# Zero-weight products of TensorE inside the value sums of the L1 attention

## What is computed

```python
qkv = hidden_states @ Wqkv                       # 512 -> 32 heads x 16 (q), 16 (k), 16 (v)
scores = einsum('bqhd,bkd->bhqk', q, k) * d**-0.5
scores = where(causal, scores + slopes * (pos_k - pos_q), -1e30)
probs = softmax(scores)
attn = einsum('bhqk,bkd->bqhd', probs, v).reshape(B, S, 512)
return attn @ Wo
```

## Time and profile before

| | |
|---|---|
| median of 3 runs | 4314.05 us (4307.27 to 4315.57) |
| the profiled execution, its own time | 4301.57 us |
| its span, first to last instruction | 4299.7 us |
| busy in the span: TensorE, VectorE, ScalarE, GpSimd | 3781.4, 2802.1, 2279.9, 1890.6 us |
| mean granted TensorE clock | 0.928 of full speed |

### The profile page before, as it was taken

One profiled execution on the slowest core, in us unless ns is written; L12 is line 12 of the kernel. 1 busy time (PEld: TensorE's weight loads), 2 busy tenths in 40 slices (PEclk: granted clock), 3 DMA queues, 4 the chain that ended last, 5 costly groups with the idle time before them and its releaser, 6 DMA issues.

```text
span 4299.7 us, 63322 instructions
## 1 busy us (share of the span) xinstructions
PE 3781.4 (88%) x21648; PEld 1877.8 (44%) x21648; DVE 2802.1 (65%) x4529; ACT 2279.9 (53%) x3945; POOL 1890.6 (44%) x1566
## 2 busy tenths in 40 slices
PE   6799987889988849999999999999999984867899
PEld 2344443223332325555455555555555552443344
DVE  6533323675567448888888898888888866565322
ACT  5522221455455546667666676667666654453222
POOL 5400000000000317778787877778787774553000
PEclk7699996789889979999999999999999997998999
DMA  3100001101000010000000000000000001012100
GB/s 109 48 1 1 0 23 27 16 1 18 16 1 1 1 57 12 21 16 13 24 1 25 12 24 13 20 18 10 27 1 24 6 25 38 23 45 67 36 10 20
DMA packets 62768, 91.28 MB, mean 21 GB/s; under 512 B 12309, under 2 KB 36392, under 8 KB 62452
## 3 DMA queue, kind: packets, MB, share of 16 engines
q1 hardware_dynamic: 62456, 87.31, 7.2%
HBM read 73.62 MB, written 6.85 MB: 19 GB/s over the span
## 4 chain that ended last, share of the span: by engine, by line
PE 65%; DVE 14%; issue 8%; ACT 6%; POOL 3%; DMA 2%; SPq 1%; DVEq 0%; POOLq 0%; ACTq 0%
PE psum L329 14%; PE psum L330 14%; PE psum L331 14%; PE psum L1370 3%; DVE arena L1519 3%; PE psum L2431 2%; PE psum L2419 2%; PE psum L1343 2%; PE psum L2427 2%; PE psum L2388 2%; PE psum L1354 2%; PE psum L2410 1%; DVE x L2116 1%; ACT xn L218 1%; PE psum L1339 1%
## 5 line engine op out<-in xcount | busy, mean ns | idle before, releaser
L329 PE MATMUL psum<-xt_hi,arena 128*128 128x512 f16 (+1 forms) x2272 | 869.9, 383 | 50.3 <-DVE arena L1509 14.2
L330 PE MATMUL psum<-xt_lo,arena 128*128 128x512 f16 (+1 forms) x2272 | 868.8, 382 | 0.0
L331 PE MATMUL psum<-xt_hi,arena 128*128 128x512 f16 (+1 forms) x2272 | 867.5, 382 | 0.0
L2214 POOL TENSOR_TENSOR arena<-arena 128x1024 f16<-128x1024 f16 x256 | 516.2, 2035 | 78.0 <-DVE arena L2026 47.1
L1288 POOL TENSOR_TENSOR rs<-sd,epsc 128x1 f32<-128x1 f32 x15 | 8.2, 548 | 1130.8 <-DVE sd L1563 1130.8
L1519 DVE TENSOR_REDUCE arena<-psum 128x1 f32<-128x512 f32 (+3 forms) x608 | 366.1, 656 | 180.7 <-PE psum L1343 179.5
L329 PE MATMUL psum<-arena 128*128 128x512 f16 (+1 forms) x1152 | 421.5, 369 | 59.0 <-DVE arena L2839 20.7
L1471 ACT ACTIVATE arena<-psum 128x512 f32<-128x512 f32 x576 | 319.7, 598 | 282.9 <-PE psum L1354 183.3
L330 PE MATMUL psum<-arena 128*128 128x512 f16 (+1 forms) x1152 | 421.1, 369 | 0.0
L331 PE MATMUL psum<-arena 128*128 128x512 f16 (+1 forms) x1152 | 420.8, 369 | 0.0
L329 PEld LDWEIGHTS psum<-xt_hi,arena 128*128 128x128 f16 x2272 | 223.9, 99 | 300.2 <-DVE arena L1505 14.6
(11 more groups left out here) (330 smaller groups left out, 7839.5 us busy)
## 6 DMA issues: line engine op xcount, KB each, us to landing
arena<-m_wi SPq DMA_DIRECT2D x64, 320.0 KB, 3.0
arena<-m_wo SPq DMA_DIRECT2D x32, 256.0 KB, 2.6
arena<-arena SPq DMA_DIRECT2D x96, 64.0 KB, 2.5
x<-L_attn_x SPq DMA_DIRECT2D x4, 1024.0 KB, 8.6
out<-x SPq DMA_DIRECT2D x4, 1024.0 KB, 4.3
arena<-gate_wT SPq DMA_DIRECT2D x16, 224.0 KB, 2.5
arena<-up_wT SPq DMA_DIRECT2D x16, 224.0 KB, 2.5
arena<-down_wT SPq DMA_DIRECT2D x14, 256.0 KB, 2.6
```

Of the source, the lines that this page charges most:

```text
L329: nc.tensor.matmul(out, lh, rh, start=start, stop=False)
L330: nc.tensor.matmul(out, lh, rl, start=False, stop=False)
L331: return nc.tensor.matmul(out, ll, rh, start=False, stop=stop)
L2214: nc.gpsimd.tensor_tensor(m4_ar[:, q], heads[q].broadcast_to([P, HG, P]), m4_le.unsqueeze(1).broadcast_to([P, HG, P]), ALU.mult).then_inc( ...
```

## The change

`add_zero(n, w)` issues n products with the zero weights `a2_z` over w columns of `a2_oh` (the output weights of the layer, any finite data would do) into the bank of the value sums, with `start=False`: they add zero to it. They are issued only while a sum is open, that is, after a value step that is not the last of its sum (`open_sums`). Ahead of each score there is one of 256 columns; ahead of a row and of an x step three of 512 columns. No position has another number of any other step, and nothing moves on another engine.

```diff
+            def add_zero(n, w):
+                for _ in range(n):
+                    nc.tensor.matmul(psum[:, 6, 0:w], a2_z, a2_oh[:, 0, 0:w], start=False, stop=True, skip_group_check=True)
+
+            open_sums = False
             for what, p, *u in STEPS2:
...
                 elif what == "row":
+                    if open_sums:
+                        add_zero(3, 4 * P)
                     e = SLOT2[what, p]
                     pe.wait_ge(a2_e, max(e, 2))
...
                 elif what == "score":
+                    if open_sums:
+                        add_zero(1, 2 * P)
                     score_unit(p, *u)
                 elif what == "value":
                     b, t = SEQ2[p]
+                    open_sums = u[0] % (t + 1) < t
...
                 elif what == "x":
+                    if open_sums:
+                        add_zero(3, 4 * P)
                     pe.wait_ge(x_norm, p + (NT * (s + 1) + 1))
```

## The result

The changed kernel takes 4376.7 us (median of 4 runs, 4366.2 to 4384.6) beside 4310.7 us for the kernel before (4 runs): a ratio of 1.0155, with a 95% interval of 1.0124 to 1.0187. It is 67 us slower. The forecast was 17 us faster, and the time lies outside the range, which ended at 4345 us.

What follows compares the result with a forecast made beforehand. TensorE was taken as busiest (89% of the stage) but slowed by half clock, its full-clock pace shared with VectorE. Terms -46 (clock) + 24 (scores) + 2 (row, x) + 3 (remaining half clock) = -17 us: median 4314 to 4297, range 4256 to 4345 us.

Steps and rivals of the forecast that it cites:

- Products ahead of scores: Added 256-column products ahead of scores: 445 at 0.108 us, bounds 0 and 48 us, half taken, +24 us.
- Rival D: Each product ahead of a score also pays its weight load: 93 us less 46 for the clock, +47, 4361 us; chance 0.06.
- Cover: Share of the products ahead of scores hidden in TensorE's slack or waits for VectorE: about half of 48 us.
- slack of 0.145 us: TensorE's spare time in each 0.60 us pair of maximum and score where VectorE sets the pace, said to cover 0.108 us.
- rival C: TensorE is the bound between its gaps, in tails' scores and dense stretches; pairs 0.70 us apart; +35, 4349 us; chance 0.20.
- Products ahead of row and x: 72 products of 512 columns, 15.5 us, mostly fill 28.2 us of waits ahead of row and x steps; +2 us taken.
- The clock: Of 218 us at half clock in the stage, two thirds, 145 us, come back at 0.32 each: -46 us.
- most begin behind a gap ahead of an x step (L1430) or a row step (L1388): Where the stage's 22 half-clock stretches were said to begin; a few behind a wait of the maxima.
- the scores around it bring more 128-row products: Near half-filled row or x gaps of 1.3 us, products ahead of scores help most clock falls go.
- Rival E: Zero-weight products leave the stage's clock where it is and only their cost is left: +34, 4348 us; chance 0.08.

Runs made afterwards that it cites:

- row and x only: The changed kernel without the products ahead of scores, leaving 72 ahead of row and x steps; 0.9968 of the kernel before, about 14 us faster.
- ahead of even scores: Kernel before plus one zero product of 64 rows (0 to 63) by 512 columns ahead of each even score, none ahead of row and x; ratio 1.0031, about +13 us.
- scores only: The changed kernel without the products ahead of row and x, leaving 445 of 256 columns ahead of scores; 1.0344 of the kernel before, about +148 us.
- with 32 columns: Kernel before plus the 445 products ahead of scores at 32 instead of 256 columns, none ahead of row and x; ratio 1.0256, about +110 us.
- row, x and odd scores: Kernel before plus the row and x products and, ahead of odd scores, products of rows 0 to 63 by 512 columns; ratio 0.9958, about -18 us.

## Why the prediction was wrong

*The step that failed* is "Products ahead of scores": "445 of 256 columns, 0.215 / 2 = 0.108 us each at full clock", of which half, 24 us, was taken. In line a product costs 0.31 us, 138 us in all, and 84 us of it were paid (the change against row and x only, at nearly equal clock). The upper bound, 48 us, was too low: it rested on the earlier trace rows, products of equal size in a row. The prediction said that no row showed a change from 51 to 128 rows, and then priced that case only in a rival. A change of size stood in the trace before all the same, right behind the earlier trace rows, from a score to a value group:

```profile
994.81 0.38 PE L1354 MATMUL psum<-arena 51*128 51x512 f16 x1
...
995.12 1.06 PE L1370 MATMUL psum<-arena 128*32 128x512 f32 x8
```

It takes 0.31 us instead of 0.22, in the median of 59 such pairs too.

*The rule weighed.* Rival D came nearest: 0.108 + 0.10 us for each in line by the weight load of the added product, 93 us, where 84 were paid. That is luck in part. It has one side of the switch where the runs show two, 0.31 us in line, and pays all of it, where three fifths were paid; and its 46 us from the clock are too many. The rule it was taken from (the Trainium skill, "TensorE: Matmul & The Clock Gate", Part 3: a load overlaps only where row groups differ) is not what decides: ahead of even scores the load ran beside a product on the same rows. The rule that bears is another one, which the prediction did not weigh: the Trainium skill, "TensorEngine Tiling (Array Packing)", Key Properties, says that changing the tiling mode drains TensorE. The trace agrees in that time is lost at each change of size, 96 and 109 ns for the two sides; the drain itself it doesn't show.

*Cover.* 84 of 138 us were paid, 61%, where the prediction had 50%. The slack of 0.145 us beside VectorE's pace is one part of the rest. The other is that the next maximum starts beside the score, which the prediction had not seen. So the mark of rival C, pairs 0.70 us apart, is not met in the dense place shown, where they are 0.62 us apart. Its claim, TensorE as the bound, holds over the stage (busy 96%). A product is dearest where few maxima stand between: 12.7 / 56 = 0.23 us in position 7, beside 0.18 us over the four positions.

*Products ahead of row and x.* Right: the waits went from 28 to 10 us, and alone these products bring 14 us.

*The clock.* The worth of a microsecond was about right (0.28 measured, 0.32 forecast). Its amount was not: 203 to 138 us of half clock, 65 us instead of 145, so -20 us instead of -46. Two readings under it failed. The first is "most begin behind a gap ahead of an x step (L1430) or a row step (L1388)". In the trace before, the longest idle time of TensorE shortly ahead of a half-clock stretch (its last 4 us) lies ahead of a maximum or its mask in 13 of the 22 cases and ahead of a row or x step in 8. The change leaves 10 stretches, 2 of them behind a row step and 7 behind a maximum: it took most of the kind that it filled, and that kind was the smaller one. The second is that the products ahead of scores would hold the clock up: "the scores around it bring more 128-row products". Alone they pulled it down, from 0.87 to 0.82. (Also, the stretch behind the stage loses no less to the clock than the stage itself: 2 x 0.04 x 2820 = 226 us beside 218.)

Put together, -20 (row and x, clock and all) + 84 (ahead of scores) = +64, the stage's 63.9 us. It adds up by construction, since row and x only is the step between the two; what stands on its own is the 0.18 us for each product at full clock, 80 us for 445. Rival E is refuted: products with zero weights do move the clock (row and x only, 0.87 to 0.91 in the stage, 0.937 to 0.943 over all executions).

## What to carry to other kernels

An added product costs what its neighbours make of it: among products on half of the array's rows a full-array one costs 0.205 us beyond its columns at full clock and parts the pairs that ran side by side, so price it from a row with that change of size (here score to value group, 0.31 us for 0.215 us of columns), not from a run of equal ones. Filling a wait that is there anyway is what paid: three products at each of 24 places ahead of waits gave 0.32%, six gave nothing, and the 445 in the stream, 84 us, lost over five times as much. If filler must stand in the stream, give it its neighbours' size on the rows they leave free, or bundle it. Before filling gaps to hold a clock up, count which gaps its falls stand behind; here most stood behind waits of the maxima, ahead of which nothing was added.

## What the hardware showed that was not expected

A switch of size costs the same 96 + 109 ns with 32, 256 and 512 columns. A weight load for the same rows overlaps the running product when both are of one size (start to start 0.22 us).

The clock is not raised by an engine that is recorded as busy: scores only had TensorE busy 98.7 of 100 us at a mean clock of 0.69, and with 32 columns the stage was at 0.76, while row and x only, less busy (90%), had 0.91. Nor does more work on half of the rows hold it down: row, x and odd scores has 223 such products more than row and x only and is at 0.93. And the two parts don't add: the row and x products are worth 14 us alone and some 70 us beside the products ahead of scores. That the stalls between sizes are what pulls the clock down fits these runs, but no run shows it by itself; it stays open.
